# The product with Wi in a recurrent gated block: whole float32 operands instead of split float32r parts

## What is computed

```python
def step(carry, xs):
    r, state = carry
    qt, kt, vt = xs                     # q = layernorm(x), k = v = context
    r = decay * r + kt * vt
    retained = (qt * r).reshape(B, D)
    inp = retained @ Wi.T + bi
    gate = jax.nn.sigmoid(inp @ Wg.T + bg)
    blended = gate * state + (1.0 - gate) * inp
    state = jnp.tanh(blended @ A.T + inp @ Bm.T)
    out = state @ Wo.T + bo
    return ((r, state), out)
...
x = x + tanh(g_xattn) * out
x = x + tanh(g_ffn) * ffn(layernorm(x))   # two products with ternary weights, relu between
```

## Time and profile before

| | |
|---|---|
| time, median of 3 runs (lowest to highest) | 314.59 us (313.75 to 315.14) |
| span of the profiled execution | 311.7 us |
| busy in the profiled execution: PE | 300.7 us, 96% |
| PEld | 274.0 us, 88% |
| DVE | 273.8 us, 88% |
| ACT | 243.9 us, 78% |
| POOL | 84.5 us, 27% |
| mean granted TensorE clock | 0.998 of full speed |

### The profile page before, as it was taken

One profiled execution on the slowest core, in us unless ns is written; L12 is line 12 of the kernel. 1 busy time (PEld: TensorE's weight loads), 2 busy tenths in 40 slices (PEclk: granted clock), 3 DMA queues, 4 the chain that ended last, 5 costly groups with the idle time before them and its releaser, 6 DMA issues. The chain is left out here.

```text
span 311.7 us, 9499 instructions
## 1 busy us (share of the span) xinstructions
PE 300.7 (96%) x3774; PEld 274.0 (88%) x3774; DVE 273.8 (88%) x805; ACT 243.9 (78%) x560; POOL 84.5 (27%) x147
## 2 busy tenths in 40 slices
PE   7989889999999999999999999999999999999995
PEld 5878778899999999999999999999999999997884
DVE  5987999999999999999999989998999998978763
ACT  4698668978878787978878787879878787857693
POOL 3533053131413214132314123132314121141230
PEclk9999999999999999999999999999999999999999
DMA  7933116142423434443414334444414224170321
GB/s 261 403 109 75 68 36 137 37 67 82 99 42 128 64 137 69 137 67 108 87 49 119 53 136 69 137 70 134 69 53 118 39 70 67 71 103 36 67 36 67
DMA packets 19564, 29.45 MB, mean 94 GB/s; under 512 B 1856, under 2 KB 10304, under 8 KB 19392
## 3 DMA queue, kind: packets, MB, share of 16 engines
q0 software_dynamic: 8720, 8.39, 19.0%
q1 hardware_dynamic: 10368, 19.93, 18.5%
q10 hardware_dynamic: 432, 0.53, 0.5%
HBM read 16.26 MB, written 4.19 MB: 66 GB/s over the span
## 5 line engine op out<-in xcount | busy, mean ns | idle before, releaser
L480 ACT ACTIVATE state<-pre_ps,sc 128x64 f32<-128x64 f32 x128 | 40.1, 313 | 40.0 <-PE pre_ps L1080 39.1
L470 ACT ACTIVATE hid<-hid_ps,b_s 128x256 f32<-128x256 f32 x120 | 50.3, 472 | 11.0 <-PE hid_ps L1119 8.6
L1119 PE MATMUL hid_ps<-xt_lo,w_q 128*128 128x256 f16 x240 | 55.5, 272 | 0.0
L1131 PE MATMUL y_ps<-w_q,h_lo 128*128 128x256 bf16 x240 | 55.5, 272 | 0.0
L1119 PE MATMUL hid_ps<-xt_hi,w_q 128*128 128x256 f16 x240 | 55.5, 272 | 0.0
L1131 PE MATMUL y_ps<-w_q,h_hi 128*128 128x256 bf16 x240 | 55.5, 272 | 0.0
L749 DVE TENSOR_TENSOR h_lo<-hid,h_hi 128x512 f16<-128x512 f32 x60 | 41.3, 688 | 5.7 <-ACT h_hi L476 5.2
L1074 PE MATMUL pre_ps<-m_hi,a_hi 128*128 128x32 f16 x508 | 42.6, 178 | 2.6 <-DVE m_hi L698 2.2
L1074 PEld LDWEIGHTS pre_ps<-m_hi,a_hi 128*128 128x128 f16 x508 | 33.5, 96 | 9.1 <-DVE m_hi L698 4.9
L1074 PE MATMUL pre_ps<-m_hi,a_lo 128*128 128x32 f16 x508 | 41.4, 176 | 0.0
L476 ACT CAST h_hi<-hid 128x512 f16<-128x512 f32 x60 | 37.1, 618 | 1.9
(11 more groups left out here) (183 smaller groups left out, 894.7 us busy)
## 6 DMA issues: line engine op xcount, KB each, us to landing
x_norm<-x_rows_in SPq DMA_DIRECT2D x16, 256.0 KB, 2.8
cx<-ctx_in SPq DMA_DIRECT2D x16, 256.0 KB, 3.4
x_res<-x_in SPq DMA_DIRECT2D x16, 256.0 KB, 3.7
x_res<-bo_g POOLq DMA_DIRECT2D x16, 256.0 KB, 4.8
x<-b_g POOLq DMA_DIRECT2D x15, 256.0 KB, 3.9
y_out<-y SPq DMA_DIRECT2D x15, 256.0 KB, 2.0
w_raw<-w_in SPq DMA_DIRECT2D x2, 512.0 KB, 7.1
w_raw<-w_in SPq DMA_DIRECT2D x1, 1024.0 KB, 9.4
```

What stands on the lines that cost most here:

```text
L470: last = nc.scalar.activation(hid[:, p % 2, u, :], hid_ps[p % 2][:, u * N:(u + 1) * N], ACT.Relu, bias=b1_s[:, 2 * p + u:2 * p + u + 1], s ...
L480: nc.scalar.activation(state[:, q[1] % 2, :, step_cols(j)], pre_ps[q[1] % 2][:, :].rearrange("p (k n) -> p k n", k=K)[:, :, step_cols(j)], ...
L1119: last = nc.tensor.matmul(hid_ps[p % 2][:, u * N:(u + 1) * N], w1_q[:, k, cut], v[:, par, k, :], start=n == 0, stop=n == len(terms) - 1)
L1131: last = nc.tensor.matmul(y_ps[:, t * D:(t + 1) * D], h[:, f, t * P:(t + 1) * P], w2_q[:, f, :], start=f == 0 and t == 0 and h is h_hi, st ...
```

## The change

`inp_product` reads `ret` and `wsq[WI]`, the transferred copy of Wi, as they are, in float32. There are four statements of a product, one for each m and k, where there were twelve. It waits for `ret_set`. The split of Wi and of the retained input goes, with its tiles and semaphores: one cast on ScalarE and one subtraction on GpSimd in the start, and in each of the sixteen calls a cast on ScalarE and a subtraction on VectorE.

```diff
             def inp_product(q):
-                pe.wait_ge(ret_hi_set, upto(q))
-                high_terms(inp_ps, wi_hi, wi_lo, ret_hi)
-                pe.wait_ge(ret_lo_set, upto(q))
-                low_terms(inp_ps, wi_hi, ret_lo).then_inc(inp_sum, 1)
+                pe.wait_ge(ret_set, upto(q))
+                for m in range(K):
+                    for k in range(K):
+                        last = nc.tensor.matmul(inp_ps[:, m * N:(m + 1) * N], wsq[WI][:, k, m * P:(m + 1) * P], ret[:, k, :],
+                                                start=k == 0, stop=k == K - 1)
+                last.then_inc(inp_sum, 1)
...
             keep_warm(WARM["ret"])
-            pe.wait_ge(pool_prep, pdone["wi_lo"])
+            pe.wait_ge(wsq_in_s[WI], 16)
             inp_product((0, 0))
...
             pool.wait_ge(xh1_set, 1)
-            whole_low("wi", wi_hi, wi_lo, WI)
             whole_low("wg", wg_hi, wg_lo, WG)
...
             square((0, 0))
-            act.wait_ge(wsq_in_s[WI], 16)
-            nc.scalar.copy(wi_hi[:, :, :], wsq[WI][:, :, :]).then_inc(act_prep, 1)
             act.wait_ge(wsq_in_s[WG], 16)
...
-            def ret_high(q):
-                act.wait_ge(ret_set, upto(q))
-                nc.scalar.copy(ret_hi[:, :, :], ret[:, :, :]).then_inc(ret_hi_set, 1)
...
-            def ret_low(q):
-                dve.wait_ge(ret_hi_set, upto(q))
-                nc.vector.tensor_tensor(ret_lo[:, :, :], ret[:, :, :], ret_hi[:, :, :].bitcast(f32),
-                                        ALU.subtract).then_inc(ret_lo_set, 1)
```

More of the change, by code:

```diff
@@ L61, in build @@
         wsq = [sb(f"wsq{n}", [P, K, D]) for n in range(5)]
-        wi_hi, wi_lo = sb("wi_hi", [P, K, D], f32r), sb("wi_lo", [P, K, D], f32r)
         wg_hi, wg_lo = sb("wg_hi", [P, K, D], f32r), sb("wg_lo", [P, K, D], f32r)
@@ L105, in build @@
         ret = sb("ret", [P, K, N])
-        ret_hi, ret_lo = sb("ret_hi", [P, K, N], f32r), sb("ret_lo", [P, K, N], f32r)
         inp = sb("inp", [P, K, N])
@@ L153, in build @@
         shifted1, negated1 = sem("shifted1"), sem("negated1")
-        ret_set, ret_hi_set, ret_lo_set = sem("ret_set"), sem("ret_hi_set"), sem("ret_lo_set")
+        ret_set = sem("ret_set")
         inp_sum, inp_set, inp_hi_set, inp_lo_set = sem("inp_sum"), sem("inp_set"), sem("inp_hi_set"), sem("inp_lo_set")
@@ L242, in build @@
         done = {name: n + 1 for n, name in enumerate(PREP)}
-        APREP = ["gates", "wi", "wg", "bm", "aw", "a", "bo_b2", "wo", "sums"]
-        PPREP = ["wi_lo", "wg_lo", "s_a", "sc"]
+        APREP = ["gates", "wg", "bm", "aw", "a", "bo_b2", "wo", "sums"]
+        PPREP = ["wg_lo", "s_a", "sc"]
         pdone = {name: n + 1 for n, name in enumerate(PPREP)}
@@ L502, in side_sign @@
                                      bias=thr[:, w:w + 1]).then_inc(act_prep, 1)
-            ret_high((0, 0))
             half_sum(0)
@@ L551, in first @@
                 tanh_step(CHUNK, 2)
-                ret_high(NEXT_CHUNK)
                 scaled_high(wo_hi, WO, S_WO)
@@ L574, in body @@
                         tanh_step(chain, j)
-                    if j == 1 and project:
-                        ret_high(project)
                     if j in HIDDEN_SLOTS and ffn:
@@ L835, in _ @@
             nc.vector.tensor_reduce(mx[:, 0:1], wsq[WA][:, :, :], AX.XY, ALU.max, apply_absolute_value=True)
-            ret_low((0, 0))
             dve.wait_ge(wsq_in_s[WO], 16)
@@ L893, in first @@
                 gated_state(CHUNK, 3)
-                ret_low(NEXT_CHUNK)
                 gated_state(CHUNK, 4)
@@ L933, in body @@
                     if j == 2:
-                        if project:
-                            ret_low(project)
                         if exists(plus(c, -3)) and peeled != NC - 1:
```

## The result

| | before | after |
|---|---|---|
| median of the runs (lowest to highest), first comparison | 314.71 us (313.75 to 315.14, 4 runs) | 317.68 us (317.40 to 319.52, 4 runs) |
| the same, second comparison | 313.65 us (313.47 to 315.25, 17 runs) | 317.84 us (317.63 to 319.39, 6 runs) |
| span of the profiled execution | 311.7 us | 315.6 us |

The ratio is 1.0125 (95% interval 1.0099 to 1.0152), in the second comparison 1.0123 (1.0095 to 1.0150): the changed kernel is slower by some 4 us. The ratio and its interval are those on record; they are not the quotients of these medians, 1.0094 and 1.0134. The first two medians lie only 3.0 us apart because three of the first four executions of before took 314.6 to 315.1 us, like those of the second comparison whose mean granted clock was 0.992 to 0.995, while the clocks of these four are not on record.

The account below looks back on a forecast made before the run. The prediction took TensorE's stream to bound the steady passes. Terms 4.06 + 0.31 - 0.10 + 0.06 gave +4.3 us on the median of 314.59, so 318.9 us, range 317.3 to 321.0, chance 0.85.

Parts of the forecast that it names:

- The bound: Steady passes: TensorE's stream sets the 17.39 us period; a nanosecond off ScalarE or VectorE is worth nothing.
- Four statements are eight products: Each call with Wi: four whole float32 statements appear as eight weight loads and eight products.
- 0.216 us a half: Each of a call's eight products, with 256 moving columns, takes 0.216 us, so a call takes 1.728 us.
- the step called the weakest: Price of a half: assumes a plain float32 product streams at the pace of line 1020's transposes, 0.83 ns a column.
- Covered loads: Calls with Wi: weight loads starting 0.12 us apart hide behind products of 0.216 us and add nothing.
- A steady call, +0.312: Each of thirteen steady calls with Wi takes 0.312 us more, in full; 4.06 us together.
- First pass +0.31, second -0.10, start +0.06: The three calls before the steady ones: full price; shorter through VectorE's lost split; low part's wait saved and spent again.
- What comes off: ScalarE's sixteen casts of 608 ns and VectorE's sixteen subtractions of 725 ns, 21 us of busy time, worth nothing.
- The sum: Whole span: 4.06 + 0.31 - 0.10 + 0.06 = +4.3 us, from 311.7 to 316.0 us.
- What lies around the span: The median of the runs stands 2.9 us above the profiled span, carried over to give 318.9 us.
- Rivals 1 to 3: Calls with Wi: halves at 0.118 us, 307.4 us (0.07); halves slower than transposes, 347 (0.02); loads not covered, 334 (0.03).
- rival 4: Lighter VectorE and ScalarE pay back the added TensorE stream, so the time stays within 1.5 us; chance 0.03.

Follow-up runs that it names:

- the kernel with the split kept: The changed kernel with the retained input's cast and subtraction put back, read by nobody: steady period 17.68 us, span 316.1 us.
- half of the outputs whole: The kernel before with output half m = 0 of the product with Wi in whole float32, m = 1 in split parts: period 17.54 us, span 315.3 us.
- half the columns: Also called the half-columns run: the changed kernel with each product with Wi cut into two of 128 columns; 1.79 us a call, period 17.74 us.
- the split product at half the columns: The kernel before with every float32r product of a call with Wi cut into two of 128 columns: 2.63 us a call, period 18.60 us.
- the relief alone: The kernel before with the retained input split only once, for the first chunk, all sixteen products reading those parts: period 17.39 us, span 311.5 us.

## Why the prediction was right, and where it was off

- *The bound.* Right. The period followed the stream of TensorE to 0.02 us in the changed kernel, the kernel with the split kept, the one with half of the outputs whole and that with half the columns, and to 1.21 us added in the split product at half the columns. The prediction's sentence that a nanosecond of stream is a nanosecond of span holds upwards as far as the runs went. Downwards, 0.57 of 0.94 us came through, which the prediction had not looked for: a constant period beside a busy TensorE shows what bounds the kernel now, and not how far a cheaper product can take it.
- *Four statements are eight products.* Right: 128 products for 64 executed statements.
- *0.216 us a half.* Right to the nanosecond, and the step called the weakest was sound: a product of plain float32 columns streams at the pace of the transposes of the earlier trace rows, 0.216 us for 256 columns beside 0.109 for 128. The upper end of 0.224 had taken over the 0.011 us of the float32r products; plain float32 does not have them.
- *Covered loads.* Right, with more room than the reason given for it: the loads of the half-columns run followed each other at 0.112 us.
- *A steady call, +0.312.* The call is 0.31 us longer from the end of the block ahead to the end of its last product, but the period grew by 0.293. Measured in the same way, the first recurrent step behind the call takes 0.291 us instead of 0.307: its first load now begins 0.22 us ahead of its product, under the last product of the call, where it began with its product before. Over thirteen calls the 0.019 us are 0.25 us that the sum had too much; 0.016 of them lie in that step, and the rest was not located.

```profile
163.22 0.10 PEld L1074 LDWEIGHTS pre_ps<-m_hi,a_hi 128*128 128x128 f16 x1
...
165.16 0.10 PEld L1054 LDWEIGHTS pre_ps<-m_hi,a_hi 128*128 128x128 f16 x1
```

- *First pass +0.31, second -0.10, start +0.06.* Measured +0.28, -0.07 and -0.05. The mechanism of the second pass is borne out by the two runs on it: the split put back takes 0.15 us, the split removed without a longer call gives 0.44. In the start the eight products filled the time of the old wait, as worked out; the block behind them began at 11.40 us, not 11.48, because the idle products ahead began at 7.82 in this execution instead of 7.89, so the sign of this small term is that of the execution and not of the change.
- *What comes off.* Worth nothing in the steady passes, as forecast. But VectorE's busy time went down by 8.7 us and ScalarE's by 9.1, not by 11 and 10. The prediction had multiplied lengths, and the records of neighbouring instructions overlap (in VectorE's rows above the residual ends at 140.80 and `m_hi` begins at 140.72), which busy time does not count twice; that this is all of the difference was not checked further.
- *The sum.* +4.3 against +3.9 between the two spans. 0.25 of the 0.4 are the shorter step above, and 0.11 the start.
- *What lies around the span.* This step failed. The prediction put 2.9 us there, from a median of 314.59 and a span of 311.7. It is 1.8 us: 317.4 beside 315.6, and 313.5 beside 311.7 in the later runs. By their times, two of the three executions behind that median were of the longer kind with the lower clock, and the median was set beside the span of an execution at 0.998. This step put the forecast 1.1 us too high and the sum 0.4; the median of the first comparison lies 0.3 above the profiled execution, which leaves the 1.2 us by which 318.9 missed 317.68. It stayed inside the forecast's range, near the low end. As a ratio, which is free of that step, the forecast was 318.9 / 314.59 = 1.0137, inside both intervals.
- *The rivals.* Rivals 1 to 3 fell with the spacing of 0.216 us, rival 4 with the run of the relief alone.

## What to carry to other kernels

Count streams, not statements: one plain float32 product of 256 columns costs two products of twice the stream, 0.43 us, while three float32r products of the same size cost 0.35 us, so the split pays on TensorE and is free as long as the engines that do the splitting have slack. At 128 columns the order turns: a call in whole float32 took 1.79 us and in split parts 2.63. Where TensorE is the bound with no wait, taking work off the other engines buys nothing, and it is worth finding out how far a cheaper product would pay (here 0.57 us a pass, of 0.94 taken out) before one is looked for. Where it stands waiting for split parts, as in the start, the whole product can win, so the choice is one per call and not one per kernel.

## What the runs showed of the hardware that was not expected

**A float32r product of 128 columns is hardly cheaper than one of 256.** Cut to 128 it takes 0.11 us instead of 0.118, so the two halves cost nearly twice the whole, and the call grew from 1.42 to 2.63 us. Whether its stream or its load sets the 0.11 us is open. Plain float32 came down with its columns (0.216 to 0.112).

**TensorE's clock fell to half in the second pass of one profiled execution.** The run with half of the outputs whole caught it. The windows of its second pass, with the granted clock as the third figure from the end:

```profile
40.00:42.00 2.00, 1.49 (x21) 0.84 (x18) 1.93 (x10) 0.90 (x3) 1.43 (x5) 1.00 0.49 139
42.00:44.00 2.00, 1.45 (x16) 1.26 (x17) 1.67 (x7) 1.88 (x5) 1.06 (x2) 0.85 0.00 0
44.00:46.00 2.00, 2.00 (x18) 1.90 (x17) 1.65 (x5) 0.14 (x1) 0.40 (x1) 0.50 0.00 0
46.00:48.00 2.00, 2.00 (x34) 1.94 (x31) 1.19 (x4) 1.68 (x6) 2.00 (x2) 0.80 0.35 49
```

And what its loads waited for ahead of it:

```profile
42.51 0.10 PEld L1079 LDWEIGHTS pre_ps<-m_hi,a_hi 128*128 128x128 f16 x1 [1.28 <-DVE m_hi L698]
```

TensorE's loads stood idle for 1.28 us up to 42.51, and the clock was at 0.50 of full speed (1.2 instead of 2.4 GHz) in the window from 44 to 46. The profiled execution of before had the same wait, with its clock at 1.00 behind it:

```profile
42.09 0.10 PEld L1074 LDWEIGHTS pre_ps<-m_hi,a_hi 128*128 128x128 f16 x1 [1.29 <-DVE m_hi L698]
...
42.00:44.00 2.00, 1.87 (x22) 1.68 (x23) 1.63 (x8) 1.59 (x4) 0.69 (x1) 1.00 0.00 0
44.00:46.00 2.00, 2.00 (x37) 1.87 (x35) 1.91 (x7) 1.22 (x5) 0.82 (x2) 1.00 0.00 0
```

The same stretch of the kernel before with nine more idle products:

```profile
40.00:42.00 2.00, 1.91 (x25) 1.55 (x25) 1.93 (x9) 1.24 (x3) 1.78 (x5) 1.00 0.49 128
42.00:44.00 2.00, 1.94 (x23) 1.59 (x22) 1.62 (x8) 1.68 (x4) 0.73 (x2) 1.00 0.00 0
44.00:46.00 2.00, 2.00 (x35) 1.87 (x34) 1.91 (x8) 1.13 (x5) 0.73 (x1) 1.00 0.00 0
```

There the clock stayed at 1.00, and none of twelve runs was slower than the rest, where five of seventeen of before were. This speaks for the idle stretch as the cause, but does not show it. If five falls were spread over the 29 runs by chance, all would lie among the seventeen about one time in twenty. The same wait went by without a fall in the profiled executions of before and of the kernel with the split kept. And in the changed kernel, whose profiled execution has its longest wait of the loads there at 0.84 us, two of ten runs had a clock of 0.995, with no trace kept of where it fell. What else must come together is open.
